# Window attention on one core: bias and masks written into PSUM by ScalarE instead of by matmuls, and value products issued ahead of the scores

## The reference: what is computed

```
x = x + attention(layernorm_c(x))            # shifted windows 7x7, 12 heads of width 8
t = x as tokens
t = t + moe(layernorm_t(t))                  # 4 experts, top 2, exact gelu, hidden 384
```

```
attn = einsum('bhwnqd,bhwnkd->bhwnqk', q, k) / sqrt(8)
attn = attn + rel_table[index]                # a bias for each head, query and key
mask[-1] += ul;  mask[:, -1] += lr            # last window row, last window column: -inf blocks
p = softmax(attn + mask);  o = einsum('bhwnqk,bhwnkd->bhwnqd', p, v)
```

## Time and profile before

| | |
|---|---|
| median of 3 runs | 6766.18 us |
| profiled execution | 6764.57 us |
| its span | 6762.7 us, mean granted PE clock 0.996 |
| PE busy | 94% of the span, 99456 matmuls |
| DVE busy | 82%, 17191 instructions |
| ACT busy | 70%, 9087 instructions |
| POOL busy | 55% |
| DMA | 37 GB/s, 13% of the engines' time |

### The profile page before, as it was taken

The page is one execution under the profiler, slowest core; times in us unless marked ns, Lnnn a source line. Parts: engine busy times, 40 slices in busy tenths (PEclk is TensorE's granted clock), DMA queues, the critical chain, the costliest instruction groups (busy, mean ns, idle before and its releaser), DMA issues.

```text
span 6762.7 us, 265902 instructions
## 1 busy us (share of the span) xinstructions
PE 6343.8 (94%) x99456; PEld 5075.1 (75%) x99456; DVE 5527.9 (82%) x17191; ACT 4718.2 (70%) x9087; POOL 3752.5 (55%) x3337
## 2 busy tenths in 40 slices
PE   5999999999999999999999999999999999999998
PEld 4777777777777777777777777777777777777776
DVE  6888888888888888888888888888888888888886
ACT  3777776777777777777777777777777777777775
POOL 3555555555555555555555555555555555555555
PEclk9999999999999999999999999999999999999999
DMA  1111111111111111111111111111111111111110
GB/s 52 37 38 36 38 37 38 36 39 36 38 36 39 37 38 36 39 37 38 36 38 37 38 37 38 36 38 37 38 36 38 36 39 36 38 37 38 36 36 20
DMA packets 168083, 251.48 MB, mean 37 GB/s; under 512 B 44498, under 2 KB 129106, under 8 KB 166738
## 3 DMA queue, kind: packets, MB, share of 16 engines
q1 hardware_dynamic: 166866, 234.70, 12.1%
HBM read 80.38 MB, written 38.54 MB: 18 GB/s over the span
## 4 chain that ended last, share of the span: by engine, by line
PE 49%; DVE 33%; issue 10%; ACT 4%; POOL 2%; SPq 1%; DVEq 1%; ACTq 0%; DMA 0%; POOLq 0%
PE ps_t L1038 10%; PE ps_o L1055 8%; DVE k_bd L728 6%; PE ps_s L1018 4%; DVE g_lo L877 4%; DVE g_hi L872 3%; PE ps_f L1129 3%; PE ps_f L1127 3%; PE ps_f L1125 3%; PE ps_s L1028 3%; PE ps_o L1064 3%; DVE s_max L734 3%; POOL rstd L428 2%; DVE stat L765 2%; PE ps_t L985 2%
## 5 line engine op out<-in xcount | busy, mean ns | idle before, releaser
L439 POOL TENSOR_TENSOR g_lo<-g_sb,g_hi 128x784 f16<-128x784 f32 x1152 | 2015.3, 1758 | 2249.1 <-DVE g_hi L872 1530.3
L532 ACT ACTIVATE g_sb<-ps_f 128x392 f32<-128x392 f32 x3072 | 1525.5, 497 | 128.1 <-PE ps_f L968 126.9
L554 ACT ACTIVATE pt_sb<-ps_t 113x588 f32<-113x588 f32 x1024 | 676.4, 661 | 1079.3 <-PE ps_t L1038 1066.3
L1129 PE MATMUL ps_f<-w_hi,g_lo 128*128 128x96 f16 x8832 | 1228.3, 206 | 0.0
L1127 PE MATMUL ps_f<-w_lo,g_hi 128*128 128x96 f16 x8832 | 1227.7, 206 | 0.0
L1125 PE MATMUL ps_f<-w_hi,g_hi 128*128 128x96 f16 x8832 | 1227.1, 206 | 0.0
L734 DVE TENSOR_REDUCE s_max<-ps_s 113x12 f32<-113x588 f32 x1024 | 788.1, 770 | 413.5 <-PE ps_s L1028 410.4
L449 POOL TENSOR_TENSOR xr<-y_gated,xr 112x192 f32<-112x192 f32 (+1 forms) x1536 | 986.0, 658 | 101.5 <-DVE xn L785 98.9
L966 PE MATMUL ps_f<-x_hi,w_hi 128*128 128x392 f16 x3072 | 1012.2, 330 | 19.5 <-issue 5.3
L968 PE MATMUL ps_f<-x_hi,w_lo 128*128 128x392 f16 x3072 | 1010.7, 329 | 0.0
L967 PE MATMUL ps_f<-x_lo,w_hi 128*128 128x392 f16 x3072 | 1010.7, 329 | 0.0
(11 more groups left out here) (133 smaller groups left out, 13713.5 us busy)
## 6 DMA issues: line engine op xcount, KB each, us to landing
k_st<-qk_hi SPq DMA_DIRECT2D x768, 49.0 KB, 1.9
q_st<-qk_hi SPq DMA_DIRECT2D x768, 49.0 KB, 2.0
xr<-x SPq DMA_DIRECT2D x224, 139.1 KB
out<-xr SPq DMA_DIRECT2D x224, 139.1 KB
xa<-x SPq DMA_DIRECT2D x224, 136.5 KB
k_st<-qk_lo SPq DMA_DIRECT2D x384, 49.0 KB, 2.1
q_st<-qk_lo SPq DMA_DIRECT2D x384, 49.0 KB, 1.9
xa<-x SPq DMA_DIRECT2D x224, 10.5 KB
```

Source lines behind the costliest of these rows:

```text
L439: nc.gpsimd.tensor_tensor(g_lo[:, slot, 0:TOK], g_sb[:, chunk, :], g_hi[:, slot, 0:TOK], ALU.subtract).then_inc(lo_done, 1)
L532: nc.scalar.activation(g_sb[:, chunk, half * STRIP:(half + 1) * STRIP], h_bank[k % 3][:, 0:STRIP], ACT.Gelu, scale=1.0 / WSCALE).then_inc( ...
L1129: ins = T.matmul(outp, g_lo[:, slot, cols], w2_hi[:, wc], start=False, stop=(c == CPE - 1), skip_group_check=True)
```

## The change

- PE: only pair 0 still gets its bias by matmuls. For pairs 1 to 7 `scores` issues the 6 key products alone, and they accumulate on what stands in `ps_s`. It waits for a new semaphore, `bias_done`, instead of `sub_done`.
- ACT: `put_bias(n)` copies a table of 113 x 588 32-bit values (bias and mask of that pair, four variants) from SBUF into `ps_s`. It waits for `sub_done` of pair n-1. It is issued ahead of `exps(0)` for pair 1, and then in each round n = 0 to 5 between `copy_pt(n)` and `exps(n+1)`, for pair n+2.
- PE: in the loop `attend(n-1)` now stands ahead of `scores(n+1)`.
- Setup: the four tables are made by DVE; the second selection matrix and the 16-bit mask table go.

```diff
+            def put_bias(a, n):
+                act.wait_ge(sub_done, at(a, N_S, n))
+                half, wr = n // 4, 2 * (n % 4)
+                variant = (1 if half == 1 and a[1] % UPI == UPI - 1 else 0) + (2 if wr == NW - 2 else 0)
+                nc.scalar.activation(ps_s[0:SPAN, 0:HEADS * NB].rearrange("p (h k) -> p h k", k=NB)[:, :, 0:WW],
+                                     biases[:, variant, :].rearrange("p (h k) -> p h k", k=WW), ACT.Copy
+                                     ).then_inc(bias_done, 1)
...
             def attention(a, b, f=None):
+                put_bias(a, 1)
                 exps(a, 0)
                 for n in range(8):
                     if n == 7 and b is not None:
                         qk_high(b, 0)
                     copy_pt(a, n)
+                    if n < 6:
+                        put_bias(a, n + 2)
                     if n < 7:
                         exps(a, n + 1)
...
                 tmp = x1_hi[:, 0:HEADS * WW]
                 fill(V.tensor_copy(tmp, offs["rel"]))
+                fill(V.tensor_tensor(bias16[NB:128, :], offs["rel"][NB:128, :], tmp[NB:128, :], ALU.subtract))
+                fill(V.tensor_copy(bias16[0:NB, :], tmp[0:NB, :]))
+                fill(V.tensor_copy(biases[:, 0, :], offs["rel"][0:SPAN, :]))
+                fill(V.tensor_tensor(biases[:, 1, :], biases[:, 0, :], offs["lr"][0:SPAN, :], ALU.add))
                 for v in range(2):
+                    fill(V.tensor_tensor(biases[:, 2 + v, :], biases[:, v, :], offs["ul"][0:SPAN, :], ALU.add))
...
             def scores(a, n):
                     pe.wait_ge(kbd_done, at(a, N_KBD, N_KBD))
                 else:
-                    pe.wait_ge(sub_done, at(a, N_S, n))
-                variant = 1 if half == 1 and a[1] % UPI == UPI - 1 else 0
+                    pe.wait_ge(bias_done, at(a, N_S - 1, n))
                 s3 = ps_s[:, 0:HEADS * NB].rearrange("p (h k) -> p h k", k=NB)
-                blocks = ((slice(0, NB), slice(0, NB)), (slice(NB, SPAN), slice(NB, SPAN)))
-                for h0, h1 in ((0, 8), (8, 12)):
-                    for rows, cols in blocks:
-                        T.matmul(s3[rows, h0:h1, 0:WW], sel16[:, cols], bias16[:, variant, h0 * WW:h1 * WW],
-                                 start=True, stop=False, skip_group_check=True)
-                    if wr == NW - 2:
-                        rows, cols = blocks[1]
-                        T.matmul(s3[rows, h0:h1, 0:WW], selB16[:, cols], ul16[:, h0 * WW:h1 * WW],
-                                 start=False, stop=False, skip_group_check=True)
+                if n == 0:
+                    for h0, h1 in ((0, 8), (8, 12)):
+                        for r0 in (0, NB):
+                            T.matmul(s3[r0:min(r0 + NB, SPAN), h0:h1, 0:WW], sel16[:, r0:min(r0 + NB, SPAN)],
+                                     bias16[:, h0 * WW:h1 * WW], start=True, stop=False, skip_group_check=True)
...
+                    if n:
+                        attend(a, n - 1)
                     if n < 7:
                         scores(a, n + 1)
-                    if n:
-                        attend(a, n - 1)
```

More of the change, by code:

```diff
@@ L134 @@
          ("w2", CHUNKS * C),
-         ("rel", HEADS * WW), ("lr", HEADS * WW), ("ul", HEADS * WW), ("sel", SPAN), ("selB", SPAN))
+         ("rel", HEADS * WW), ("lr", HEADS * WW), ("ul", HEADS * WW), ("sel", SPAN))
 N_CONST = 5
@@ L168, in build @@
         sel16 = sb("sel16", [128, SPAN], F16)
-        selB16 = sb("selB16", [128, SPAN], F16)
-        ul16 = sb("ul16", [128, HEADS * WW], F16)
-        bias16 = sb("bias16", [128, 2, HEADS * WW], F16)
+        bias16 = sb("bias16", [128, HEADS * WW], F16)
+        biases = sb("biases", [SPAN, 4, HEADS * WW])
         wqk_hi = sb("wqk_hi", [128, 2 * C], F16)
@@ L255, in build @@
         q_in, k_in = sem("q_in"), sem("k_in")
-        max_done, sub_done = sem("max_done"), sem("sub_done")
+        max_done, sub_done, bias_done = sem("max_done"), sem("sub_done"), sem("bias_done")
         rec_done = sem("rec_done")
@@ L639, in setup @@
                 fill(V.tensor_copy(sel16[:, :], offs["sel"]))
-                fill(V.tensor_copy(selB16[:, :], offs["selB"]))
-                fill(V.tensor_copy(ul16[:, :], offs["ul"]))
                 for src, hi, lo in (("wqk", wqk_hi, wqk_lo), ("wv", wv_hi, wv_lo),
@@ L1224, in _layout @@
     lr, ul = np.zeros((128, HEADS, WW), f), np.zeros((128, HEADS, WW), f)
-    lr[0:WW] = np.where(late(col)[:, None] != late(col)[None], MASKED, 0.0)[:, None, :]
-    ul[0:WW] = np.where(late(row)[:, None] != late(row)[None], MASKED, 0.0)[:, None, :]
-    sel, selB = np.zeros((128, SPAN), f), np.zeros((128, SPAN), f)
+    lr[0:WW] = lr[NB:SPAN] = np.where(late(col)[:, None] != late(col)[None], MASKED, 0.0)[:, None, :]
+    ul[NB:SPAN] = np.where(late(row)[:, None] != late(row)[None], MASKED, 0.0)[:, None, :]
+    sel = np.zeros((128, SPAN), f)
     q = np.arange(WW)
@@ L1231, in _layout @@
             sel[k0 + q, m0 + q] = 1.0
-    selB[q, NB + q] = 1.0
     parts = {"wqk": _rows(wqk), "wv": _rows(wv), "wg": _rows(wg), "w1": _rows(w1b), "b2": b2r,
              "rel": rel.reshape(128, -1), "lr": lr.reshape(128, -1), "ul": ul.reshape(128, -1),
-             "sel": sel, "selB": selB}
+             "sel": sel}
     parts["w2"] = w2.reshape(EXPERTS, CPE, 128, C).transpose(2, 0, 1, 3).reshape(128, CHUNKS * C)
```

## The result

The changed kernel takes 7241.95 us (median of 4 runs, 7238.52 to 7247.43) against 6766.04 us before (median of 4 runs, one more than above): a ratio of 1.0704, 95% interval 1.0686 to 1.0723. The forecast was 7178 us, with a range up to 7240. Direction and place were right, the time lies 2 us outside the range, and the distance of 64 us from the forecast is small by luck, since two errors partly cancel: the loops cost about 112 us less than forecast, and the clock of TensorE, which the forecast took as full, fell and cost about 160 us.

What follows compares the result with a forecast made beforehand. A loop through TensorE and VectorE was taken as the bound, not TensorE's volume: 0.75 + 0.62 + 0.35 + 1.51 = +3.23 us per unit, times 128 = +413 us on 6764.57, giving 7178 us; range 7045 to 7240.

Steps and rivals of the forecast that it cites:

- the loop: Maximum, normalising, `turn_o`, `attend`, key products, next maximum: 3.44 us per pair in four steps, +0.75 us per unit.
- rival 1: TensorE's volume of work decides, not the loop: removed matmuls save 311 us, giving 6454 us; chance 7%.
- first step: From pair 0's row maximum to pair 1's, nothing hides the bias copy: 3.08 us instead of 2.46, +0.62.
- second step: From pair 1's row maximum to pair 2's, exponential of pair 0 behind bias copy: 3.28 us instead of 2.93, +0.35.
- save step: From pair 5's row maximum to pair 6's, `attend(4)` awaits the save of outputs: 4.56 us instead of 3.05, +1.51.
- M(7): Start of pair 7's row maximum (M(n): pair n's); behind it the old order was to stay, with no bias copy.
- rival 4: Emptier stretches lower TensorE's clock; a twentieth of the time at 1.2 GHz adds at most 317 us: 7495 us; 2%.
- rival 3: ScalarE's bias copy into PSUM is slow, 1.2 us: 1.40 us more per unit, 179 in all, 7357 us; 4%.
- Rival 2: Rest of the unit makes up some loss, at most 193.9 us: 6984 us, some 7080 at half effect; 8%.

Runs made afterwards that it cites:

- e9: Kernel before with `attend` ahead of `scores` and five filling matmuls ahead of the wait of `attend(4)`, bias and masks still by matmuls: 7256.67 us, ratio 1.0723.
- e4: Changed kernel with five filling matmuls ahead of the wait of `attend(4)`, whose results nothing reads: 7077.97 us, ratio 1.0458.
- e1: Changed kernel with `attend(n-1)` back behind `scores(n+1)`, the bias copies staying on ScalarE: 6823.59 us, ratio 1.0084.
- e8: Changed kernel with VectorE's `normalise_o(n-1)` ahead of `softmax_pair(n+1)`: 7008.87 us, ratio 1.0361.
- e3: Changed kernel with only `attend(4)` put back behind `scores(6)`: 7094.84 us, ratio 1.0482.
- e5: Changed kernel with `attend` back behind `scores`, and `put_bias(n+2)` ahead of `copy_pt(n)` on ScalarE: 6910.60 us, ratio 1.0209.

## Why the prediction was right or wrong

**Right: the loop is the main cause.** The two-by-two of order and place of the bias, all at a clock of 0.994 or more (the two of the new order with fillers, which cost 13 us in e9), is: old order, matmuls 6766; old order, ScalarE 6824; new order, matmuls 7257 (e9); new order, ScalarE 7078 (e4). The order costs 491 us with the one and 254 us with the other. The nine groups of matmuls removed are worth 179 us in the new order, where they stand in the loop, and -58 us in the old one, where e1's ScalarE order makes a loop of its own. None of the four shows the 311 us of rival 1.

**Mis-sized: the loop, 3.44 forecast, 3.33 measured.** The step from `attend` to the key products is 0.57 us, not the 0.66 that I took from `attend` to the transposes; what follows `attend` decides when it can start. The rest is 0.02 us in two hand-overs. Over four steps that is 0.44 us.

**Mis-sized: first step, 2.89 for 3.08.** The copy is 0.66, not 0.68; ScalarE started it 0.04 us behind the subtraction, not 0.12 as the first exponential of a unit, and PE followed 0.05 behind the copy, not 0.15. The 0.12 belongs to that one instruction: in e8 the exponentials that wait for a subtraction start 0.03 to 0.04 us behind it. The second step was 3.23 for 3.28.

**Mis-sized: the save step, 4.36 for 4.56.** ScalarE started the bias copy 0.09 us earlier than forecast, and the key products came 0.57 us behind `attend` instead of 0.66. Its mechanism is as forecast: copy, exponential, save, `attend`. In sum the loops cost 2.35 us per unit instead of 3.23, 301 instead of 413 us; e4 measures 312. The stretch behind M(7) was rightly left alone: from there to the next unit it is 30.56 us against 30.54 before.

**Failed: the clock.** The step that failed is the one that held it at full speed. It was rival 4, at 2%, with "if a twentieth of the time ran at 1.2" as a price; it was 84 of 126 units, for 3.4 or 10.2 us each, and filling the idle time gave 164 us back (e4). I took the earlier trace rows, where 94% busy goes with a full clock, as evidence for 88% busy. What I did not do is look at where the idle time would gather: my own sum had `turn_o(3)` at 2.07 and `attend(4)` at 3.42 us behind M(5), with only one transpose between them. The trace has 0.65 and 0.96 us of idle time there, 0.3 us apart. The Trainium skill (TensorE: Matmul & The Clock Gate, A second HAM failure mode: psum-queue depth-cycling) had the warning that frequent short idle times between groups of matmuls can make the clock go up and down. The trace agrees with its direction: a mean clock of 0.956 with the idle time ahead of `attend(4)` and 0.994 with it filled. The forecast range reached 7240 on the way up because of rival 3, a slow copy, which the 0.664 us of the line group rules out. Rival 2 (time made up later) has nothing for it: 30.56 against 30.54.

Open: why the clock falls in 84 units and holds in 42 that idle alike, why it stays down for 3.4 us in some and 10.2 in others, and why it falls in e3 with the save wait moved. No run tests what separates these units.

## What to carry to other kernels

Before moving work ahead of something on an in-order engine, find the loop that sets the spacing and ask whether the moved work was beside it; taking 0.27 us of matmuls out of a loop while putting 0.57 us in is a loss, however busy the engine looks (the whole change cost 312 us at an equal clock, with the removed matmuls counted in). A small gain was there in the old order, but it took three steps on the engine that took the work over: the bias copy ahead of `copy_pt` (22 us at an equal clock), the save ahead of the exponential (62 us), and the first pair, where nothing hides the copy, back on TensorE (58 us). Where an edit gathers idle time on TensorE in one place, check the granted clock of the stretches behind it, not the mean.

## What the runs showed of the hardware

- More work can be faster: 640 matmuls put into idle time gave 164 us back through the clock (0.956 to 0.994).
- The fall is to 0.50, for 3.4 us (46 units of the changed kernel) or 10.2 us (38 units), and it comes behind the idle stretch ahead of `attend(4)`. The length of one idle piece does not decide it: 0.96 us there brought it in 84 of 126 units (changed kernel) and 1.10 us in 66 (e5), 0.54 us did not in e1 (mean clock 0.994) and 0.55 us did in 88 (e3, 0.972). Idle pieces of about 0.5 us ahead of `turn_o`, 640 in the run, did not bring it by themselves (e4, 0.994).
- The same 24 value products took 0.57 us until the key products could start behind them (weights of 49 columns) and 0.66 us until the 16-bit projection of unit b could (weights of 96 columns), both in the changed kernel; ahead of the transposes (113 columns) it is 0.66 us in the kernel before. The cause was not tested.
- ScalarE writes 113x588 32-bit values from SBUF into PSUM in 0.664 us, the same as the 0.661 us out of PSUM; the engine starts it 0.04 us behind the instruction that it waits for. The Trainium skill (ScalarE: Activation LUTs, Step-by-step: what each stage is for) calls PSUM the faster target. No run here has the same work with both targets: of the nearest rows of this run, the exponential into SBUF takes 0.691 us, 0.03 more, and the copy out of PSUM into SBUF no more than the copy into PSUM. So the trace leaves it open.
